# A delta-rule attention kernel on one core: the scores' mask moved into the decay factors, one PSUM bank per use, and new durations for the planner of the instruction order

## The reference, cut to what matters

```python
def step(S, xs):
    qt, kt, vt, gt, bt = xs
    S = S * jnp.exp(gt)[..., None, None]
    kv = jnp.einsum('bhk,bhkv->bhv', kt, S)
    delta = (vt - kv) * bt[..., None]
    S = S + jnp.einsum('bhk,bhv->bhkv', kt, delta)
    o = jnp.einsum('bhk,bhkv->bhv', qt * scale, S)
    return (S, o)
```

## Time and profile before

| | us |
|---|---|
| median of 3 runs (4457.74 to 4464.0) | 4459.4 |
| the profiled execution's own time | 4440.69 |
| its span, first to last instruction | 4438.9 |
| TensorE busy in the span | 4027.7 |
| VectorE busy | 3351.7 |
| ScalarE busy | 2328.1 |
| GpSimd busy | 1800.7 |

### The profile page before, as it was taken

One profiled execution on the slowest core, in us unless ns is written; L12 is line 12 of the kernel. 1 busy time (PEld: TensorE's weight loads), 2 busy tenths in 40 slices (PEclk: granted clock), 3 DMA queues, 4 the chain that ended last, 5 costly groups with the idle time before them and its releaser, 6 DMA issues. The chain is left out here.

```text
span 4438.9 us, 85469 instructions
## 1 busy us (share of the span) xinstructions
PE 4027.7 (91%) x29688; PEld 3205.8 (72%) x29688; DVE 3351.7 (76%) x6260; ACT 2328.1 (52%) x5908; POOL 1800.7 (41%) x2000
## 2 busy tenths in 40 slices
PE   7999999998898998889998989998898888898987
PEld 6888887886677776767777767777776677676764
DVE  6666666664877888787888887888877778877785
ACT  1222222222656666566666666666665666665663
POOL 2232322231344344443444444434444435554554
PEclk9999999999899999899999999999999999999998
DMA  4111111112433344434444444444444444444453
GB/s 135 54 45 29 39 45 45 30 31 80 122 100 98 104 109 110 115 101 115 115 126 106 112 131 129 132 115 122 108 115 115 127 125 139 132 122 130 129 136 88
DMA packets 836205, 450.59 MB, mean 102 GB/s; under 512 B 490560, under 2 KB 749120, under 8 KB 835776
## 3 DMA queue, kind: packets, MB, share of 16 engines
q1 hardware_dynamic: 817632, 412.09, 34.7%
q10 hardware_dynamic: 18144, 33.04, 2.6%
HBM read 276.06 MB, written 168.85 MB: 100 GB/s over the span
## 5 line engine op out<-in xcount | busy, mean ns | idle before, releaser
L1294 PE MATMUL bank<-xtile,wt 128*128 128x256 f32 x3584 | 956.5, 403 | 36.3 <-ACT stage L1325 17.1
L1294 PEld LDWEIGHTS bank<-xtile,wt 128*128 128x128 f32 x3584 | 675.1, 199 | 179.6 <-issue 77.9
L1766 ACT ACTIVATE xyinv<-bank 128x512 f16<-128x512 f32 x768 | 444.9, 592 | 335.0 <-PE bank L1709 332.9
L2023 PE MATMUL bank<-wot,xnt 128*128 128x512 f32 x1024 | 541.0, 626 | 17.8 <-DMA xnt<-x_scratch 16.8
L1294 PE MATMUL bank<-wt,xtile 128*128 128x256 f32 x1792 | 455.3, 388 | 1.8 <-ACT zs L1325 1.5
L1742 DVE TENSOR_TENSOR wlev<-bank,mask 128x256 f16<-128x256 f32 x768 | 307.9, 411 | 175.0 <-PE bank L1709 173.1
L561 PE MATMUL bank<-hb,wt 128*128 128x128 f32 x2816 | 376.1, 277 | 8.3 <-DVE part L601 5.7
L1294 PEld LDWEIGHTS bank<-wt,xtile 128*128 128x128 f32 x1792 | 326.4, 191 | 63.1 <-issue 24.6
L1659 POOL TENSOR_TENSOR ltm<-ltm,mask 128x512 f32<-128x512 f32 x128 | 179.7, 1404 | 470.5 <-DVE ltm L1647 470.4
L1709 PEld LDWEIGHTS bank<-xyinv,lth 128*128 128x128 f16 x3584 | 204.5, 101 | 221.9 <-issue 93.4
L561 PEld LDWEIGHTS bank<-hb,wt 128*128 128x128 f32 x2816 | 350.1, 194 | 17.5 <-issue 7.2
(11 more groups left out here) (238 smaller groups left out, 8977.9 us busy)
## 6 DMA issues: line engine op xcount, KB each, us to landing
xtile<-xt_scratch SPq DMA_DIRECT2D x128, 256.0 KB, 3.9
v_scratch<-vraw SPq DMA_DIRECT2D x64, 512.0 KB, 3.9
vtok<-v_scratch SPq DMA_DIRECT2D x512, 64.0 KB, 2.4
x_scratch<-tq SPq DMA_DIRECT2D x508, 64.0 KB, 1.8
xnt<-x_scratch SPq DMA_DIRECT2D x508, 64.0 KB, 2.5
grows<-row_scratch ACTq DMA_DIRECT2D x126, 256.0 KB, 3.8
part_scratch<-prow SPq DMA_DIRECT2D x96, 256.0 KB, 2.4
prow<-part_scratch SPq DMA_DIRECT2D x96, 256.0 KB, 3.2
```

Of the source, the lines that this page charges most:

```text
L1294: i = pe.matmul(b[:, r * QCOLS:(r + 1) * QCOLS], lhs, rhs, start=p in FIRST and r == 0 and k == 0, stop=k == KH - 1, skip_group_check=True)
L1766: act.activation(dst, b_inv[p][:].rearrange("p (a h b s) -> p a h b s", a=2, h=HEADS, s=z), ACT.Copy).then_inc(s[f"xy_sb{p}"], 1)
L2023: i = pe.matmul(b_o[:], xnt[:, c % 2, h], wot[:, h], start=(h == 0), stop=(h == GV - 1))
```

## The change

Four things are changed together.

1. **The mask of the scores.** `dve_scores`, its tile `kqm` and the semaphore `kq_sb` are gone. `dve_lower` and `dve_attend` read the scores straight from PSUM, in the new bank `b_kq`. The entries on the wrong side of the diagonal are made zero by the decay factors instead: the scan starts at -300 (`FAR`), each head's row of log decays begins with -300 (a GpSimd memset and a ScalarE copy one column shorter in the feed-forward part), and its mask has a zero on the diagonal and ones elsewhere, so that sums left of the diagonal are -300 or less and their exponential is nothing. The factor 64 that the first mask held is added as a logarithm to the gate (`G_LNB`), and `act_eps` divides by it again. `pe_scores` of a unit now waits for `dve_lower` and `dve_attend` of the unit before.
2. **The diagonal.** `pool_unit` is an `affine_select` of one input that writes 64 where row and column agree, where it was a subtraction of a mask.
3. **The banks.** Products have two fixed banks, `b_x` and `b_w`, in place of three that rotate; scores and output projection have one each. The product order is P1, P2, P6, P5, P7, P4, P3 for all quads, and P1 of the next quad comes behind P3 instead of ahead of P4. P5 waits for the addition of P2 (same bank), P1 for the copy of P4.
4. **The planner's durations.** In `TAKES` these are longer (us): GpSimd sums of an x tile 4.9 to 5.6 and of weights 4.9 to 6.0, `unit` 1.16 to 1.35, `low` 1.16 to 1.25, `kend` 1.25 to 1.37, `gated` 1.27 to 1.40, `norm` 2.42 to 2.90; ScalarE `lead` 0.64 to 0.72, `keys`, `queries` and `norm` 1.27 to 1.95, `decay` 1.15 to 1.58, `query` 1.15 to 1.46; VectorE `conv` 0.64 to 0.80, `decay` 1.22 to 1.25, `lower` and `attend` 0.69 to 0.70, `start` 0.42 to 0.50, `error` 1.04 to 1.19. TensorE's are as they were.

```diff
-    m[:, M_OFF] = 1.0 - np.eye(P)
-    m[:, M_NEG] = -SCALED * np.eye(P)
+    m[:, M_OFF:] = (1.0 - np.eye(P))[:, None, :]
...
-    m[:, M_LT] = SCALED * (r[:, None] < r[None, :])
-    m[:, M_LE] = r[:, None] <= r[None, :]
-    m[:, M_PAST:] = (r[:, None] < r[None, :])[:, None, :]
...
-                link(dve.tensor_scalar(gout[:, u % 2, :, :, G_LNB, :], soft[:, 1].rearrange("p j (g h) -> p j g h", g=GROUPS), -1.0, None, ALU.mult))
+                link(dve.tensor_scalar(gout[:, u % 2, :, :, G_LNB, :], soft[:, 1].rearrange("p j (g h) -> p j g h", g=GROUPS), -1.0, math.log(SCALED), ALU.mult, ALU.add))
...
+                pool.memset(grow[:, :, 0:1], -FAR).then_inc(s["set"], 1)
...
-        kqm, gam = sb("kqm", [P, 2 * KPB, P]), sb("gam", [P, HEADS, P])
+        gam = sb("gam", [P, HEADS, P])
...
-        b_o, _, b_i0, b_i1, b_s0, b_s1 = bank[2:]
-        rotated = (bank[0], bank[1], bank[3])
+        b_x, b_w, b_kq, b_o, b_i0, b_i1, b_s0, b_s1 = bank
...
-            b = x_bank(t) if p in PX else y_bank(t) if p in PY else w_bank(t)
+            b = b_x if p in PX else b_w
             if r == 0:
                 if p == "P1":
                     pe.wait_ge(s[f"x_in{par}"], 64 * (q // 2 + 1))
                     pe.wait_ge(s[f"w{kind}_in"], 64 * (group(q) + 1))
                     if t:
-                        pe.wait_ge(s["qa_sb"], 3 * (t - 1) + 1)
+                        pe.wait_ge(s["qc_sb"], 4 * t)
                 elif p == "P2":
                     if t:
                         pe.wait_ge(s["qa_sb"], 3 * t)
                 elif p == "P5":
-                    pe.wait_ge(s["xsum"], 4 * (q + 1))
-                    pe.wait_ge(s["wsum"], 4 * (group(q) * NQ + j + 1))
-                    if t:
-                        pe.wait_ge(s["qc_sb"], 4 * t)
+                    pe.wait_ge(s["qa_sb"], 3 * t + 1)
                 elif p == "P3":
                     pe.wait_ge(s["qa_sb"], 3 * t + 2)
                 else:
+                    if p == "P6":
+                        pe.wait_ge(s["xsum"], 4 * (q + 1))
+                        pe.wait_ge(s["wsum"], 4 * (group(q) * NQ + j + 1))
                     pe.wait_ge(s["qc_sb"], 4 * t + PX.index(p))
...
             if n:
-                pe.wait_ge(s["kq_sb"], n)
-            if n > LEAD:
-                pe.wait_ge(s["po_sb"], n - LEAD)
+                pe.wait_ge(s["lt_sb"], n)
+                pe.wait_ge(s["pt_sb"], n)
             pe.wait_ge(s["k_in"], K_IN * tile + (1 + HALVES) * KEYS_IN)
             pe.wait_ge(s["silu"], tile * N_SILU + 2)
             for j in range(KPB):
                 h = m * KPB + j
-                i = pe.matmul(b_o[:].rearrange("p (t h c) -> p t h c", t=2, h=KPB)[:, :, j], kt[:, tile % 2, cc, h], kqt[:, tile % 2, :, cc, h], start=True, stop=True)
+                i = pe.matmul(b_kq[:].rearrange("p (t h c) -> p t h c", t=2, h=KPB)[:, :, j], kt[:, tile % 2, cc, h], kqt[:, tile % 2, :, cc, h], start=True, stop=True)
...
-        def dve_scores(dve, n):
-            dve.wait_ge(s["kq_ps"], n + 1)
-            if n:
-                dve.wait_ge(s["lt_sb"], n)
-                dve.wait_ge(s["pt_sb"], n)
-            dve.tensor_tensor(kqm[:].rearrange("p (t h) c -> p t h c", t=2), b_o[:].rearrange("p (t h c) -> p t h c", t=2, h=KPB),
-                              mask[:, M_LT:M_LE + 1, :].unsqueeze(2).broadcast_to([P, 2, KPB, P]), ALU.mult).then_inc(s["kq_sb"], 1)
...
-            dve.tensor_tensor_scan(gam[:].rearrange("p h c -> p (h c)"), grows[:, n % 2], mask[:, M_PAST:, :].rearrange("p h c -> p (h c)"), 0.0, ALU.add, ALU.mult).then_inc(s["sum_sb"], 1)
+            dve.tensor_tensor_scan(gam[:].rearrange("p h c -> p (h c)"), grows[:, n % 2], mask[:, M_OFF:, :].rearrange("p h c -> p (h c)"), -FAR, ALU.add, ALU.mult).then_inc(s["sum_sb"], 1)
...
-        scored = lambda lo: kqm[:, lo:lo + KPB].unsqueeze(2).broadcast_to([P, KPB, REP, P])
+        scored = lambda t: b_kq[:].rearrange("p (t h c) -> p t h c", t=2, h=KPB)[:, t].unsqueeze(2).broadcast_to([P, KPB, REP, P])
...
-            pool.tensor_tensor(ltm[:], ltm[:], mask[:, M_NEG, :].unsqueeze(1).broadcast_to([P, HEADS, P]), ALU.subtract).then_inc(s["lti_sb"], 1)
+            pool.affine_select(ltm[:], ltm[:], [[0, HEADS], [1, P]], ALU.not_equal, SCALED, base=0, channel_multiplier=-1).then_inc(s["lti_sb"], 1)
...
-            act.activation(reps[:], split(b_s0), ACT.Copy).then_inc(s["e_sb"], 1)
+            act.activation(reps[:], split(b_s0), ACT.Copy, scale=1.0 / SCALED).then_inc(s["e_sb"], 1)
...
-                pe.wait_ge(s["kq_sb"], min(c + LEAD + 1, UNITS))
...
-            yield 0, "P1"
             for t in quads:
-                yield from ((t, p) for p in (("P5", "P2", "P6", "P7") if QUADS[t % NQ] == "v" else ("P5", "P6", "P2", "P7")))
-                if t + 1 in quads:
-                    yield t + 1, "P1"
-                yield from ((t, p) for p in ("P4", "P3"))
+                yield from ((t, p) for p in ("P1", "P2", "P6", "P5", "P7", "P4", "P3"))
```

72 lines of the change are left out of this document (34 added, 38 removed).

## The result

The kernel after takes **4149.7 us** (median of 3 runs, 4146.3 to 4155.4) against 4459.4: a ratio of 0.9305, 95% interval [0.9284, 0.9326], or 309.7 us less. The forecast was 4275 us, 184 less. The direction and most of the mechanism were right, the size was off by 126 us. The result lies 0.3 us under the range's low end of 4150, less than its own three runs differ; the other form in which the range was given, a gain of up to 320 us, would reach to 4139.

The account below looks back on a forecast made before the run. TensorE was taken to bound the kernel, with its idle time and clock in the attention to be won: 124 + 10 + 62 - 12 = 184 us off the median 4459.4 gives 4275 us, range 4150 to 4415.

Parts of the forecast that it names:

- TensorE's idle time in the attention: Of 341.8 us idle: 124 won from starved stretches, 10 from short chain waits, 12 lost to two product banks.
- the clock: Attention, after starved stretches: 103 us lost to half-rate work at the low clock, 60% of it, 62 us, won.
- What bounds it: TensorE sets the attention's time; the static order starves it about once a tile, where VectorE is full.
- The first rival: Attention: long waits go, but short waits at very many chain steps cost 107 us, giving 4380 us; chance 0.20.
- the last: Product banks: late ScalarE copies stall TensorE on the x bank, 230 us lost, giving 4505 us; chance 0.07.
- The order: Attention: fewer long runs of chain steps win three quarters of 166 us of starved idle time, 124 us.
- The reading of one stretch: One starved stretch: TensorE waits 2.21, 1.42 and 0.96 us while VectorE does mask product and convolution taps first.
- The matmuls "the same in number and shape": TensorE's matmuls are unchanged in number and shape; no term of the sum was given for them.
- Two product banks: P4 right behind P7 in one bank, ScalarE's copy between: 25 us at most, 12 us taken as lost.
- At nothing: `pe_out` no longer waiting for the scores: Output projection freed from waiting for the scores: priced at no time.
- VectorE's work: Removed masked copy and cheaper PSUM reads: 166 us less busy time, direct effect 22 us where VectorE is full.
- The select: GpSimd's diagonal select: 1.35 us each, bounds 1.10 and 1.40, hidden by VectorE's work before the chain's `start`.

Follow-up runs that it names:

- e10: The kernel before with the scores' lead over the output projection in their shared bank cut from 3 units to 2: 4716 us.
- e6: The kernel before with the mask and diagonal changes alone, banks and planner durations as before: 4213 us.
- e5: The kernel before with two fixed product banks and the new product order, scores and output projection still sharing a bank: 4427 us.
- e3: The kernel before with the bank change and product order alone, masked scores in SBUF and old durations kept: 4248 us.
- e13: The kernel after with the old planner durations, and each unit's decay scan made to wait for its scores again: 4190 us.
- e7: The kernel after, same order, with one unused VectorE product of the scores' bank and a mask added per unit: 4167 us.
- e8: The kernel after, same order, with one unused GpSimd operation added ahead of each of the 128 selects: 4147 us.
- e4: The kernel before with the bank change, product order and new planner durations, masked scores in SBUF kept: 4198 us.
- e2: The kernel after with the planner's durations of before: 4140 us.
- e15: The kernel after with two buffers for the decay factors `gam` and the scan in a lane of its own: 4144 us.
- e16: The kernel after with the old planner durations, two buffers for `gam` and the scan in its own lane: 4170 us.
- e17: The kernel after with the planner's DMA landing time raised from 2.4 to 3.3 us: 4115 us.
- e18: The kernel after with the old planner durations and the planner's DMA landing time raised from 2.4 to 2.9 us: 4140 us.
- e9: The kernel before with the scores' lead over the output projection in their shared bank raised from 3 units to 6: 4306 us.
- e14: The kernel before with the mask and diagonal changes alone and a lead of 4 units instead of 3: 4283 us.
- e12: The kernel before with the decay scan put ahead of the masked copy of the scores in VectorE's build lane: 4319 us.

## Why the prediction was off

The sum, term by term, against the two profiled executions:

| us | forecast | measured |
|---|---|---|
| TensorE's idle time in the attention | 124 + 10 - 12 | 175 |
| the clock | 62 | 82 |
| other busy time of the same matmuls | 0 | 33 |
| sum, the difference of the spans | 184 | 290 |
| before's median over its profiled execution | 0 | 19 |

**What bounds it: right.** The idle time lay in starved stretches of a static order. Seven of eight went, the short waits of the chains did not take their place, and the clock followed. The first rival (the idle time moves) and the last (the x bank: 16.5 us of waits, not 100) did not come.

**The order, 124 us: the term of the sum that failed.** The starved part fell from 61.3 to 6.1 us between 1600 and 2800 us, 90% where I took three quarters: 149 us by the same scale of 166. The rest of the idle time fell too, from 64.3 us in 1040 to 61.5 in 1180, 6.2 to 5.2% of the time; on the 176 us I took 10, and it was some 25. Together 175 us; forecast 134, less 12. These 53 us are half of the 106 by which the sum is short.

**The reading of one stretch: wrong in part.** I put the waits of the earlier trace rows down to VectorE. Its longest, 2.21 us, was for ScalarE's `xyinv`, and ScalarE stood in the exponentials of `gam` and the table load ahead of them:

```profile
2388.73 1.28 ACT L1632 ACT_TABLE_LOAD   x1
2390.03 0.40 ACT L1632 ACTIVATE gam<-gam,gts 128x128 f32<-128x128 f32 x1
...
2390.34 0.97 ACT L1632 ACTIVATE gam<-gam,gts 128x128 f32<-128x128 f32 x3
2391.21 0.57 ACT L1766 ACTIVATE xyinv<-bank 128x512 f16<-128x512 f32 x1
```

The waits of 1.42 and 0.96 us were VectorE's. So the static order starved TensorE through both engines, and taking work from VectorE could cure only a part.

**The clock, 62 us of at most 103: right in its rate, on too little idle time.** I had read 64% busy from one 12-us window behind a starved stretch and scaled it to all of the low clock; over all 351 us it is 78%, so 137 us were to be had, not 103. The clock gave back 82. Across the experiments it goes with the idle time: summed over each kernel's stretches at 1.2 GHz as above, TensorE is busy for 439 us in e10 and 135 in e6. Half of the difference to before is 82 us lost on 156 more of idle time in e10, 70 won on 146 in e6, and 82 on 175 in after, 0.47 to 0.53 us for each; the forecast had 62 on 124.

**The matmuls "the same in number and shape": 33 us that were taken as nothing.** Busy time fell by 115 us for the same matmuls, and the clock is 82 of them. An estimate for the rest: the profile counts a 128x256 matmul as busy for 379 ns, while in a row the next starts 216 ns after it, so each time TensorE falls idle some 163 ns are counted that overlap in a row. TensorE fell idle 461 times in the attention before and 228 times after; 233 times 0.163 is 38 us. In e10 (605 times) the same reckoning gives 23 us where 32 are left beside the clock, in e6 (351 times) 18 where 14 are left.

**Two product banks, a loss of 12 us: wrong in sign.** e5 has these banks and their order alone and is 0.4% faster. The waits for the x bank did grow, by 6 us (10.4 to 16.5); the rest of the order made up for them.

**"At nothing: `pe_out` no longer waiting for the scores": the reason that failed.** I priced this edge by the wait it removes, and in a static order a bond has no wait to show: the planner had already arranged the program around it. e3 and e5 differ by it and its counterpart alone (the scores no longer wait for the projection): 4248 and 4427 us, 179 us for what I had put at nothing. My order term held its effect unnamed, since I measured the finished order; so the sum was less wrong than its reasons. The same goes for the scan that no longer stands behind the scores, 50 us by e13, which the prediction doesn't name.

**VectorE's work, 166 us of busy time, 22 us of time.** In all VectorE fell by 120 us, since the scan rose from 1263 to 1343 ns and `errh` from 508 to 701 (35 us of the 46; the rest is spread). The removed copy's share, put back in e7, costs 17 us: a low price was right. The Trainium skill (VectorE: DVE Perf Modes, Rules for kernel authors) advises a copy to SBUF ahead of many reads; here two direct reads took 0.67 us each after, 1.35 us a unit, against 2.43 us for the copy and two reads of SBUF in e3, so for two reads the direct way was the cheaper, as the rows had said.

**The select: hidden, right; 1.35 us: wrong.** It takes 0.67 us on the mean, under both bounds. e8 puts 0.64 us back per unit (mean) and is level with after.

**Durations.** I read the new order as the work of all edits; the table turned out to be worth 57 us alone, some 50 beside the banks (e4 against e3) and nothing beside the rest (e2), though with two buffers it is 26 us (e15 against e16). e17, the fastest of all, has the new table and e18 the old one, but with landings of 3.3 and 2.9 us, so they don't tell which table is the better.

## What to carry to other kernels

Where a planner writes the order, a shared buffer costs what it forbids the planner, and no wait in the trace shows it: price a bond by changing it by one step (lead 2, 3, 6 gave 4716, 4449 and 4306 us), not by the stalls at its semaphore, and look first at the end that the planner itself reckons for the changed order. Ask of each lane whether a step that needs nothing yet stands behind one that waits for data. When the order is free, what comes late next can be on a queue that nobody looked at, here the one that issues the DMAs; and a count of long runs, which moved with the time in e10, e9 and e3, says nothing on that (e14: 4 runs, 4283 us; e12: 26 runs, 4319 us). Don't scale a share from one window where the trace lets you sum over all of them (64% and 78% here).
